# TensorE's first FFN products issued ahead of the scan part of each slot, in a fused scan and mixture-of-experts kernel

## What is computed

```python
def ssd_scan(x, dt, B_in, C_in, A_log):          # step over chunks
    lcs = jnp.cumsum(dt_c * A, axis=1)
    M = jnp.exp(jnp.where(mask, diff, -jnp.inf))
    G = jnp.einsum('blhn,bihn->bhli', C_c, B_c)
    intra = jnp.einsum('bhli,bihp->blhp', M * G, x_c)
    inter = jnp.einsum('blh,blhn,bhpn->blhp', jnp.exp(lcs), C_c, h)
...
sh = jax.nn.relu(jnp.einsum('bsd,ndf->bsnf', x, sw1) + sb1)
shared = (jnp.einsum('bsnf,nfo->bsno', sh, sw2) + sb2).sum(axis=2) / NS
rh = jax.nn.relu(jnp.einsum('bsd,edf->bsef', x, rw1) + rb1)
eo = jnp.einsum('bsef,efo->bseo', rh, rw2) + rb2
...
x = x + _L0_attn_ref(_layernorm(x), ...)
x = x + _L0_ffn_ref(_layernorm(x), ...)
```

## Times and profile before

| | us |
|---|---|
| median of 3 executions | 649.76 |
| their range | 648.73 to 651.51 |
| the profiled execution, its own time | 651.84 |
| its span in the trace | 650.1 |
| TensorE busy in it | 618.2 |
| VectorE, ScalarE, GpSimd busy | 455.3, 361.5, 179.0 |
| mean granted TensorE clock, of full | 0.986 |

### The profile page before, as it was taken

How to read it: one execution, slowest core, us unless ns; L and a number is a source line. 1 busy time by engine, 2 the same in 40 slices (tenths; PEclk the granted TensorE clock), 3 DMA queues, 4 the chain that set the end, 5 groups by cost and what they waited for, 6 DMA issues and landing times.

```text
span 650.1 us, 12252 instructions
## 1 busy us (share of the span) xinstructions
PE 618.2 (95%) x4152; PEld 463.5 (71%) x4152; DVE 455.3 (70%) x1121; ACT 361.5 (56%) x793; POOL 179.0 (28%) x243
## 2 busy tenths in 40 slices
PE   6998989999999999999999999999999999999995
PEld 5676867777677777777677776777677866768663
DVE  4989676776687776776867866877767766655553
ACT  3764566637764567547566376546575476542441
POOL 4084104421143211530145211531133411241011
PEclk8999899989999999999999999999999999999998
DMA  6200000000100001000000001000010000000000
GB/s 208 70 19 1 1 1 18 2 1 1 33 2 1 2 0 35 1 2 0 5 27 0 0 0 32 0 0 0 0 32 0 1 1 17 1 1 2 17 0 16
DMA packets 12728, 8.90 MB, mean 14 GB/s; under 512 B 1642, under 2 KB 11284, under 8 KB 12692
## 3 DMA queue, kind: packets, MB, share of 16 engines
q1 hardware_dynamic: 12048, 8.27, 4.2%
q10 hardware_dynamic: 644, 0.17, 0.2%
HBM read 6.33 MB, written 2.10 MB: 13 GB/s over the span
## 4 chain that ended last, share of the span: by engine, by line
PE 61%; DVE 22%; issue 7%; ACT 6%; POOL 2%; DMA 1%; DVEq 0%; POOLq 0%; SPq 0%; ACTq 0%
PE bank L364 8%; PE bank L366 6%; PE bank L365 6%; PE bank L600 5%; PE bank L491 5%; PE bank L601 4%; PE bank L602 4%; DVE act_l L1241 3%; PE bank L524 3%; PE bank L509 3%; PE bank L542 3%; PE bank L468 2%; PE bank L519 2%; PE bank L533 2%; PE bank L478 2%
## 5 line engine op out<-in xcount | busy, mean ns | idle before, releaser
L1241 DVE SCALAR_TENSOR_TENSOR act_l<-bank,act_h 128x512 fp32r<-128x512 f32 x192 | 131.4, 688 | 130.1 <-ACT act_h L843 128.7
L843 ACT ACTIVATE act_h<-bank 128x512 fp32r<-128x512 f32 x192 | 117.1, 610 | 109.1 <-PE bank L366 105.3
L1472 POOL TENSOR_TENSOR late<-late 128x512 f32<-128x512 f32 x32 | 46.4, 1451 | 205.4 <-DVE late L1249 205.4
L364 PE MATMUL bank<-fTl,w1h 128*128 128x512 f32 x192 | 90.0, 469 | 8.1 <-DVE act_l L1241 5.7
L600 PE MATMUL bank<-act_l,w2h 128*128 128x512 f32 x192 | 78.3, 408 | 6.7 <-DVE late L1249 6.2
L867 ACT ACTIVATE decay<-bank,lneg 128x128 f32<-128x128 f32 x256 | 69.6, 387 | 14.5 <-PE bank L468 14.5
L366 PE MATMUL bank<-fTh,w1h 128*128 128x512 f32 x192 | 75.9, 395 | 0.0
L365 PE MATMUL bank<-fTh,w1l 128*128 128x512 f32 x192 | 75.8, 395 | 0.0
L601 PE MATMUL bank<-act_h,w2l 128*128 128x512 f32 x192 | 75.4, 393 | 0.0
L602 PE MATMUL bank<-act_h,w2h 128*128 128x512 f32 x192 | 75.3, 392 | 0.0
L1459 POOL TENSOR_TENSOR xw<-xs,decay 128x128 f32<-128x128 f32 x48 | 19.5, 405 | 180.7 <-ACT decay L867 123.3
(11 more groups left out here) (198 smaller groups left out, 1194.8 us busy)
## 6 DMA issues: line engine op xcount, KB each, us to landing
x_in<-L_attn_hidden_dram SPq DMA_DIRECT2D x8, 256.0 KB, 3.1
out_dram<-late SPq DMA_DIRECT2D x8, 256.0 KB, 2.9
late<-L_ffn_sw_dram SPq DMA_DIRECT2D x2, 512.0 KB, 5.7
late<-L_ffn_rw_dram SPq DMA_DIRECT2D x1, 1024.0 KB, 6.1
CT<-L_attn_w_in_proj_dram SPq DMA_DIRECT2D x1, 772.0 KB, 7.2
b_dt<-L_attn_b_dt_dram ACTq DMA_DIRECT2D x1, 128.0 KB, 5.4
w_out_raw<-L_attn_w_out_proj_dram SPq DMA_DIRECT2D x1, 128.0 KB, 6.3
d_col<-L_attn_D_dram SPq DMA_DIRECT2D x8, 0.1 KB, 3.0
```

Source lines behind the costliest of these rows:

```text
L364: mm(dst, stat_h, mov_l, start=True, stop=False)
L843: nc.scalar.activation(act_h[:, b % RING, :], HID[b % 2][:], ACT.Relu).then_inc(act_h_ready, 1)
L1241: v_.scalar_tensor_tensor(act_l[:, r, :], HID[b % 2][:], 0.0, f(act_h[:, r, :]), ALU.max, ALU.subtract)\
L1472: g.tensor_tensor(acc, acc, term, ALU.add).then_inc(acc_ready, 1)
```

## The change

The call of `first` moves ahead of everything else in its slot, apart from the filler products of `keep_busy`, in all slots but slot 4, where block 0 of a sequence starts. Nothing is added or taken away, on TensorE or elsewhere; no wait and no tile changes. The orders of ScalarE, VectorE, GpSimd and the DMA queues stay as they are.

```diff
                     if is_seq(s, 1) and i in (0, 1, 3):
                         keep_busy(FOUT, 4)
+                    if i != LATE and (new := block_at(i, prev, older)):
+                        first(*new)
                     if prev is not None:
                         if i == 5:
                             gate(prev)
...
                     if older is not None and i == 7:
                         out_transposes(prev, older)
-                    if new := block_at(i, prev, older):
+                    if i == LATE and (new := block_at(i, prev, older)):
                         first(*new)
                     if prev is not None and i == LATE - 1:
                         f_transposes(s, prev)
```

## The result

| | before | after |
|---|---|---|
| median, us (4 executions each) | 649.96 | 672.64 |
| their range | 648.73 to 651.51 | 670.83 to 673.15 |
| profiled execution | 651.84 | 673.15 |
| mean granted TensorE clock in it | 0.986 | 0.989 |
| one body (s = 4) | 75.16 | 78.08 |

The ratio is 1.034, with a 95% interval of 1.031 to 1.037. The changed kernel is 3.4% slower, where 669.5 us, or 3.0%, was forecast.

What follows compares the result with a forecast made beforehand. TensorE was not taken as the only bound: VectorE and ScalarE set slots 3 to 9, TensorE the rest from slot 10. Six bodies at 2.85 us plus 2.45 for s = 1 gave 19.6, median 669.5 us, range 657 to 677.

Steps and rivals of the forecast that it cites:

- Slots 0 to 4: F 22 waits 1.4 us for act_low, mostly absorbed; later f_transposes delay ScalarE's queue and S 0: +0.4 us a body.
- Slot 9: F 5 waits 1.7 us for block 3's act_low, with projection 13 and lcs still to do: +1.3 us a body.
- Chunks 0 to 2: Scan parts start an F later; act_lows for F 10, F 13, F 16 come near the need: +0.15 us, bounds 0 and 0.7.
- S 16 and S 19: S 16 waits for routed_out, delayed by later segments: +0.65 us; S 19 for block 19's act_low, behind output scaling: +0.35.
- only slot 9 counts: Rival: queues have more slack, terms at the relu, S 16 and S 19 vanish; 7 x 1.3 = 9, 659 us; chance 0.16.
- Faster: Rival: earlier F means earlier relu, and the four old waits go; 7 x 1.9 = 13, 636 us; chance 0.04.
- no change: Rival: gaps in slots 2 and 9 are absorbed by slack behind them; 650 us; chance 0.04.
- the one at the new waits: Rival: TensorE's clock falls at the gaps in slots 2 and 9; 21 us more, 690 us; chance 0.03.
- more falls at the ends: Rival: the clock also falls at the ends of bodies 2 to 7; 6 x 1.6 = 10, 679 us; chance 0.08.
- The signs: Expected profile: body of 78 us; TensorE idle about 1.4 at F 22, 1.6 at F 5, 0.5 at S 16, short at S 19.

Runs made afterwards that it cites:

- The fastest kernel: Kernel before with store and block 3's act_low ahead of top_two, F 6 ahead of l_transposes, routed_out ahead of block 1's act_low: 648.47 us, ratio 0.997.

## Why the prediction was right, and where it was not

**The mechanism and the sum.** A body got 2.92 us longer, 2.85 were foretold. The body for s = 1 got 2.63 longer from F 5 on to S 19 (2.45 foretold), and the two bodies without a scan kept their length. 2.63 + 6 x 2.93 = 20.2 of the 21.3 us of the two profiled executions. The rest, some 1.1 us, is the clock: ends 3 and 7 fell in the trace of after, end 1 in that of before, 1.1 to 1.65 us each, and the opening differs by a few tenths. The medians differ by 22.7, for the same reasons as far as the profiles tell.

**Slots 0 to 4, right (0.4; 0.39).** F 22 waits 1.39 us, 0.02 farther from the body's start than before. F 0 came 0.08 later than F 22's shift (309.72 against 301.21 + 8.43), where 0.1 to 0.2 was foretold, fTh 0.69 (307.12; 0.67 foretold), and relu 0.33. The rows of ScalarE in after:
```profile
307.12 0.60 ACT L792 ACTIVATE fTh<-bank 128x512 fp32r<-128x512 f32 x1 [3.33 <-PE bank L549]
...
310.08 1.09 ACT L808 COPY BT<-bank 128x512 f32<-128x512 f32 x2
311.02 0.65 ACT L845 ACTIVATE act_h<-bank 128x512 fp32r<-128x512 f32 x1
```
The relu's idle of 0.21 is gone, but the queue took in 0.36 of the 0.69 us and not 0.21: the relu now starts 0.15 before the copy in front of it ends (311.17). Behind it another 0.06 came on, so the term came out right by a somewhat different way than the one worked out. F ahead in slots 0 to 3 alone gave +0.37.

**Slot 9, too large (1.3; 1.05).** The wait of 1.74 and its releaser came as worked out. I then charged 0.70 for projection 13, 0.51 for lcs and 0.1 for the switch. The rows show 1.50 from F 5 to lcs and 0.36 from lcs to S 3. The 0.51 had been read between the starts of lcs and F 5 in the kernel before, where a fresh start behind lcs's wait is in it, and I added the 0.1 on top. That the term exists and is the largest is shown from both sides: not moving F 5 gives back 1.41, and a sooner act_low 1.96 in the changed kernel.

**Chunks 0 to 2, too small (0.15; 0.54).** The bound of 0.7 holds, the choice near zero didn't. Of the 0.54, 0.18 lies at l_transposes and S 4, where I had written that F 6 fills "most" of the wait and then charged nothing for what it doesn't fill: 0.31 us of idle. 0.22 lies between S 7 and S 8, in chunk 0, where I had found the act_low within 0.1 us of the need; the rest is in hundredths. The act_low of block 8, for which F 10 waits, ends at 339.41, and F 10 starts at 339.47. S 7's last product starts at 339.14, and products that follow at once start 0.23 apart, so F 10 is 0.10 late, and it then pays 0.1 for a fresh start. On VectorE and on TensorE:
```profile
338.72 0.69 DVE L1243 SCALAR_TENSOR_TENSOR act_l<-bank,act_h 128x512 fp32r<-128x512 f32 x1 [3.98 <-ACT act_h L845]
...
339.47 0.50 PE L364 MATMUL bank<-fTl,w1h 128*128 128x512 f32 x1
```
Slots 12 to 23 alone cost 1.22, of which S 16 and S 19 took 0.94 in after, so some 0.3 belongs to the chunks.

**S 16 and S 19, right (0.65 and 0.35; 0.68 and 0.26).** F 17 alone, moved ahead of segments, gave 0.61. On VectorE, routed_out ends at 366.47 + 0.74 = 367.21, and S 16 starts at 367.27:
```profile
366.47 0.74 DVE L1251 SCALAR_TENSOR_TENSOR late<-bank,cols,late 128x512 f32<-128x512 f32 x1
```

**The rivals.** That only slot 9 counts is refuted: with slot 9 in its old place a body is still 1.49 us longer, and the time 14.5 us (664.16 - 649.68). Faster and no change are refuted by the result. Of the two clock rivals, the one at the new waits did not come true in the changed kernel: behind all 13 waits at F 22 and F 5 of the bodies for s = 1 to 7 (1.2 to 1.8 us) TensorE ran at full clock. The windows of 3 us behind the two of s = 4:
```profile
302.10:305.10 3.00, 2.99 (x19) 2.58 (x20) 2.96 (x8) 1.23 (x2) 0.45 (x1) 1.00 0.00 0
326.10:329.10 3.00, 3.00 (x15) 2.56 (x16) 0.83 (x3) 1.29 (x5) 0.00 (x0) 1.00 0.00 0
```
As a mechanism it is not refuted: in the experiments the clock fell behind two waits of 1.37 us and at one of 2.45 and one of 2.47, as shown above. The other rival, more falls at the ends, is there in small: one more, of about a microsecond. The end of body 3 in after, output projection and the clock around it:
```profile
294.94 3.66 PE L542 MATMUL bank<-w_out,yT 128*128 128x128 f32 x16
```
```profile
294.00:298.00 4.00, 4.00 (x24) 4.00 (x24) 0.66 (x2) 0.00 (x0) 2.23 (x2) 0.62 0.01 4
```

**The signs.** What the changed profile was to show came: the waits at F 22, F 5, S 16 and S 19, and none at F 23, F 0 and lcs. Not on the list were the growth at S 0, from 0.66 to 1.06, and the 0.31 at l_transposes.

**The distance.** The forecast of 669.5 is 3.1 us below the median. For the profiled execution 671.4 was foretold and 673.15 measured, so that 1.75 of it is in the walk: 0.5 in six bodies (0.08 each, since +0.39 in the chunks and -0.25 in slot 9 nearly cancel, which is luck), 0.2 in the body for s = 1, and about 1 for the clock. The other 1.4 us come from going over to medians: the profiled execution of before was 1.9 us above its median, that of after 0.5 above its own.

## What to carry to other kernels

On an engine that runs in order, work in front of a wait covers it and work behind it does not, so before you move a call forward, write down for each call what it waits for, when that ends, and which work it now leaves behind its wait; here a move that adds no instruction cost 3.4%. The one place where moving F forward paid was where another instruction's release needed cover (l_transposes, 1.00 us of wait against 0.30). And when a wait is taken away, look for the next release in the same stretch before you count the gain: 0.66 us at S 0 came back at lcs, 0.37 at lcs came back as 0.61 at l_transposes.

## What the runs showed of the hardware

TensorE's clock fell from 2.4 to 1.2 GHz at the ends of bodies, at a place where TensorE had no idle gap of more than 0.3 us in the 5 us before: behind 16 products of one column, within 16 products of 128. It did so at 26 of the 98 ends (1 to 7) in the fourteen traces; a fall cost 1.0 to 1.7 us, because the output projection took 3.0 to 3.7 us and not 2.0. Which ends fall differs between executions. The fastest kernel showed four of seven, the one with three products of 512 columns between the two steps none, and so did the one with F ahead in slots 9 and 10. One trace of each is too little to name a cause: what decides about an end stays open.

Behind idle gaps it fell more rarely. Between the opening and the last body the fourteen traces hold 55 waits of TensorE of 1.2 to 1.9 us, and it fell behind two of them, both of 1.37 us, at lcs with routed_out ahead. It fell at both of the longer ones, 2.45 and 2.47 us. What sets those two of 1.37 us apart is not shown.

Two operations that each read two SBUF tiles, one on VectorE and one on GpSimd, stretch the one that starts second, by 0.83 us on GpSimd or 0.60 on VectorE. That is nearly the whole of the overlap: the addition starts 0.25 us behind a step of 1.22, so that 0.97 of it is left, and the step starts 0.56 behind an addition of 1.30, so that 0.74 is left. The second one thus hardly moves until the first is done, and the order of two such operations decides which engine pays.
